# Window routing of a fused four-layer network: sums of the raw input, and the choice of key blocks moved into the qkv products

## The reference

```python
# xn = groupnorm of x with groups of 4 channels: xn = x * A + B, A and B per image and channel
proj = xw @ W_qkv + b_qkv                  # xw: xn in 7 x 7 windows of 8 x 8 pixels
q_win, k_win = mean of q, mean of k        # one vector of 128 per window: 49 x 128
lepe = depthwise_conv3x3(v_img) + lepe_b
logit = einsum('npc,nqc->npq', q_win * SCALE, k_win)      # 49 x 49
_, r_idx = top_k(logit, 4)                 # for each window the 4 windows whose keys it sees
attn = softmax(q * SCALE @ k[r_idx])       # 8 heads of 16 channels, 64 x 256 per window
out = (attn @ v[r_idx] + lepe) @ W_o + b_o
```

## Time and profile before

| | us |
|---|---|
| median of 3 runs | 3797.24 (3796.34 to 3798.78) |
| profiled execution | 3793.72 |
| its span (first to last instruction) | 3792.0 |
| PE busy | 3522.8 (93%) |
| DVE busy | 2374.0 (63%) |
| ACT busy | 2142.8 (57%) |
| POOL busy | 1655.4 (44%) |
| POOL L1508 idle before it, released by the DMA row<-ix | 303.6 |

### The profile page before, as it was taken

The page is one execution under the profiler, slowest core; times in us unless marked ns, Lnnn a source line. Parts: engine busy times, 40 slices in busy tenths (PEclk is TensorE's granted clock), DMA queues, the critical chain, the costliest instruction groups (busy, mean ns, idle before and its releaser), DMA issues. The chain is left out here.

```text
span 3792.0 us, 107529 instructions
## 1 busy us (share of the span) xinstructions
PE 3522.8 (93%) x31974; PEld 2993.2 (79%) x31974; DVE 2374.0 (63%) x6251; ACT 2142.8 (57%) x5921; POOL 1655.4 (44%) x2575
## 2 busy tenths in 40 slices
PE   6989898989989898969999999999999969979999
PEld 4656565656656565659999999999999969979998
DVE  4868687777868686853333333333333349988898
ACT  4969788787879797954443333333333324435554
POOL 2636364554636363730003333333334436646665
PEclk8999999999999999989999999999999989989999
DMA  6232222323132323211110000000002100000000
GB/s 213 71 96 74 90 80 75 87 61 110 49 113 58 108 63 98 73 66 50 50 55 1 0 0 0 0 0 0 0 6 61 61 26 1 1 14 35 35 35 34
DMA packets 202875, 194.44 MB, mean 51 GB/s; under 512 B 35744, under 2 KB 191136, under 8 KB 199456
## 3 DMA queue, kind: packets, MB, share of 16 engines
q1 hardware_dynamic: 171168, 177.15, 15.0%
q10 hardware_dynamic: 31360, 12.87, 1.2%
HBM read 123.30 MB, written 66.58 MB: 50 GB/s over the span
## 5 line engine op out<-in xcount | busy, mean ns | idle before, releaser
L196 PE MATMUL bank<-h,w_hh 128*128 128x128 f32 x8032 | 933.9, 275 | 0.0
L196 PEld LDWEIGHTS bank<-h,w_hh 128*128 128x128 f32 x8032 | 917.2, 192 | 0.0
L241 ACT ACTIVATE h<-bank,bg 128x128 f32<-128x128 f32 x1008 | 370.0, 367 | 818.7 <-PE bank L196 818.6
L1579 ACT ACTIVATE Pr<-bank,nmx 128x256 f32<-128x256 f32 x1568 | 722.6, 477 | 122.4 <-DVE nmx L1682 108.0
L1516 POOL TENSOR_TENSOR Pr<-Pr,rden 128x768 f32<-128x768 f32 x392 | 574.7, 1466 | 383.3 <-DVE rden L1749 383.3
L1682 DVE TENSOR_REDUCE nmx<-bank 128x1 f32<-128x256 f32 x1568 | 557.0, 416 | 210.1 <-PE bank L1854 206.4
L287 DVE SCALAR_TENSOR_TENSOR inp<-bank,b_in,tz 128x256 f32<-128x256 f32 x196 | 85.8, 479 | 698.2 <-ACT tz L224 698.2
L1508 POOL COPY kg<-kT 128x64 f32 x1568 | 312.6, 243 | 392.4 <-DMA row<-ix 303.6
L1865 PE MATMUL bank<-ident,Pr 128*128 128x128 f32 x3136 | 450.5, 285 | 3.7 <-POOL Pr L1516 2.1
L1588 ACT ACTIVATE PT<-bank 128x512 f32<-128x512 f32 x784 | 427.3, 604 | 39.7 <-PE bank L1865 36.6
L1854 PE MATMUL bank<-kg,qT 32*128 32x256 f32 x3136 | 399.8, 440 | 31.6 <-POOL kg L1508 22.9
(11 more groups left out here) (261 smaller groups left out, 6500.2 us busy)
## 6 DMA issues: line engine op xcount, KB each, us to landing
v_rows<-v_padded SPq DMA_DIRECT2D x168, 232.0 KB, 3.4
vg<-v_windows SPq DMA_DIRECT2D x1176, 32.0 KB, 2.1
first_gates<-gate_sums SPq DMA_DIRECT2D x28, 512.0 KB, 2.6
gate_sums<-first_gates SPq DMA_DIRECT2D x28, 512.0 KB, 3.5
v_padded<-vpad SPq DMA_DIRECT2D x56, 232.0 KB, 2.4
X<-in_x SPq DMA_DIRECT2D x8, 1568.0 KB, 15.1
vg<-v_windows ACTq DMA_DIRECT2D x392, 32.0 KB, 2.2
x_backup<-X SPq DMA_DIRECT2D x8, 1568.0 KB, 6.0
```

The source lines that it names most:

```text
L196: ins = pe.matmul(bank[m][:, tt * COLS:(tt + 1) * COLS], w_hh[:, k, m * 128:(m + 1) * 128], prev[:, k, :], start=False, stop=(k == NH - 1) ...
L241: act.activation(h[:, 2 * q + tt, m, :], bank[m][:, tt * COLS:(tt + 1) * COLS], ACT.Tanh, bias=bg[:, 0, m:m + 1]).then_inc(s_h, 1)
L1579: act.activation(Pr[:, par, j, :], bank[j][:, 0:KEYS], ACT.Exp, bias=nmx[:, par, j:j + 1], accum_out=den[:, par, j:j + 1])\
```

## The change

- The window sums are taken from the raw image X by DVE (into `xraw`), seven blocks in turns 0 to 3 (`SUMS_AT`), and made into sums of the normalised input by one operation with A and 64 B in turn 3. ACT no longer waits for the sum of a block before it overwrites `xb`.
- The two products of the sums stand in turn 4, in unused columns of the k and v banks, their bias additions on DVE in the same turn; the logits' product, scaling, top 8 and positions stand in turn 5.
- SP issues the DMA of the positions at the head of its turn 6.
- Behind the turns, lepe 0 waits only for block 5's evacuation; scores(0) stand ahead of lepe 1; on ACT the copy of lepe 1 stands behind the exps of window 0.
- `VAR_AT` is 41 instead of 40.

```diff
+            SUMS_AT = {0: (0, 1), 1: (2, 3), 2: (4, 5), 3: (6,)}
+            SUMS_BLOCK, LOGITS_BLOCK = 4, 5
-            MEAN_AT, VAR_AT = 39, 40
+            MEAN_AT, VAR_AT = 39, 41
...
 # SP, in the turns
+                            if b == LOGITS_BLOCK + 1:
+                                sp.wait_ge(s_tk, n * 3 + 4)
+                                sp.wait_ge(s_kg, (n * P2) + 1)
+                                sp.wait_ge(s_Tc, (n * P2) * 2 + 1)
+                                sp.dma_start(row[0:1, :], ix[:, 0:TOPK]).then_inc(s_row, 16)
...
 # ACT
-                            if b >= 2:
-                                act.wait_ge(s_qs, n * NBLK + b - 1)
...
+                        first_lepe(0)
...
                         exps(0, 0)
+                        first_lepe(1)
...
 # DVE, in the turns
-                            dve.wait_ge(s_xb, n * NBLK + b + 2)
-                            dve.tensor_reduce(xsum[:, b * NWIN:(b + 1) * NWIN], xb[:, par, :]
-                                              .rearrange("p (w k) -> p w k", k=W2), AXX, ALU.add).then_inc(s_qs, 1)
+                            for k in SUMS_AT.get(b, ()):
+                                dve.tensor_reduce(xraw[:, k * NWIN:(k + 1) * NWIN],
+                                                  xblk(n, k).rearrange("p (r w c) -> p w r c", r=ROWS, c=WIN),
+                                                  mybir.AxisListType.XY, ALU.add).then_inc(s_qs, 1)
+                            if b == SUMS_BLOCK - 1:
+                                dve.wait_ge(s_id, n * IN_DVE + IN_DVE)
+                                dve.tensor_scalar(B64[:], Bb[:, bass.ds(n, 1)], float(W2), None, ALU.mult).then_inc(s_xs, 1)
+                                dve.wait_ge(s_xs, n * 2 + 1)
+                                dve.wait_ge(s_qs, (n + 1) * NBLK)
+                                dve.tensor_scalar(xsum[:], xraw[:], A[:, bass.ds(n, 1)], B64[:, 0:1], ALU.mult, ALU.add)\
+                                    .then_inc(s_xs, 1)
...
+                            if b == SUMS_BLOCK:
+                                for i, sums in enumerate((qs, ks)):
+                                    dve.wait_ge(s_wp, n * 2 + 2)
+                                    dve.tensor_scalar(sums[:], bank[1 + i][:, BLK:BLK + P2], b64[:, i:i + 1], None, ALU.add)\
+                                        .then_inc(s_ws, 1)
+                            if b == LOGITS_BLOCK:
+                                dve.wait_ge(s_lg, n + 1)
+                                dve.tensor_scalar(lg[:], bank[6][0:P2, BLK:BLK + P2], QSCALE / (W2 * W2), None, ALU.mult)\
+                                    .then_inc(s_tk, 1)
+                                dve.wait_ge(s_tk, n * 3 + 2)
+                                dve.max(m8[:], lg[:]).then_inc(s_tk, 1)
                             dve.tensor_scalar(vpad[...], ...).then_inc(s_v, 1)
+                            if b == LOGITS_BLOCK:
+                                dve.wait_ge(s_tk, n * 3 + 3)
+                                dve.wait_ge(s_row, n * 16 + 16)
+                                dve.max_index(ix[:], m8[:], lg[:]).then_inc(s_tk, 1)
...
 # PE, in the turns: q product, then
+                            if b == SUMS_BLOCK:
+                                pe.wait_ge(s_xs, n * 2 + 2)
+                                pe.matmul(bk[:, BLK:BLK + P2], w_qkv[:, 0:C], xsum[:], start=True, stop=True).then_inc(s_wp, 1)
                             pe.matmul(bk[:, 0:BLK], w_qkv[:, C:2 * C], xs, start=True, stop=True).then_inc(s_pk, 1)
+                            if b == SUMS_BLOCK:
+                                pe.matmul(bv[:, BLK:BLK + P2], w_qkv[:, C:2 * C], xsum[:], start=True, stop=True)\
+                                    .then_inc(s_wp, 1)
+                            if b == LOGITS_BLOCK:
+                                pe.wait_ge(s_ws, n * 2 + 2)
+                                pe.matmul(bv[0:P2, BLK:BLK + P2], qs[:], ks[:], start=True, stop=True).then_inc(s_lg, 1)
...
 # PE, behind the turns
+                        pe.wait_ge(s_V, n * NBLK + NBLK)
                         for i in range(6):
                             lepe(0, i // 2, i % 2, bank[7])
...
+                        pe.wait_ge(s_v, n * NBLK + NBLK)
+                        pe.wait_ge(s_V, n * NBLK + NBLK + 1)
                         scores(0, 0)
+                        pe.wait_ge(s_tk, n * 3 + 2)
+                        for i in range(6):
+                            lepe(1, i // 2, i % 2, bank[6])
                         scores(1, 1)
```

More of the change, by code:

```diff
@@ L1251, in program @@
             s_vst = [sem("v_stored_even"), sem("v_stored_odd")]
-            s_qs, s_bq = sem("window_sums"), sem("query_bias_ready")
+            s_qs, s_bq = sem("raw_window_sums"), sem("query_bias_ready")
+            s_xs = sem("window_sums_scaled")
             s_wp, s_ws = sem("window_sums_product"), sem("window_sums_ready")
@@ L1278, in program @@
             b64 = sb("bias_sums", [C, 2])
+            xraw = sb("raw_sum", [C, P2])
             xsum = sb("window_sum", [C, P2])
+            B64 = sb("shift_sums", [C, 1])
             ident = sb("ident", [C, C])
@@ L1421, in _ @@
                                 passed(sp)
+                            if b == LOGITS_BLOCK + 1:
+                                sp.wait_ge(s_tk, n * 3 + 4)
+                                passed(sp)
+                                sp.wait_ge(s_kg, (n * P2) + 1)
+                                passed(sp)
+                                sp.wait_ge(s_Tc, (n * P2) * 2 + 1)
+                                passed(sp)
+                                sp.dma_start(row[0:1, :], ix[:, 0:TOPK]).then_inc(s_row, 16)
                             sp.wait_ge(s_v, n * NBLK + b + 1)
@@ L1436, in _ @@
                                     stack(n, b - 2, dy)
[L1438 to L1445, removed]
                         sp.wait_ge(s_vst[0], n * (STORED * 4) + STORED * 4 + 16)
@@ L1597, in _, with first_lepe @@
                         act.wait_ge(s_o, n * P2 + 1)
-                        for b in range(2):
+                        def first_lepe(b):
                             act.wait_ge(s_lp, n * NBLK + b + 2)
                             act.activation(by_row(lp[:, b, :]), bank[7 - b][:, 0:BLK], ACT.Copy).then_inc(s_le, 1)
+                        first_lepe(0)
                         act.wait_ge(s_vst[0], n * (STORED * 4) + STORED * 4 + 16)
@@ L1656, in image @@
                             dve.wait_ge(s_pv, n * NBLK + b + 1)
+                            if b == SUMS_BLOCK:
[8 more added lines that the diff above has]
+                                dve.wait_ge(s_tk, n * 3 + 2)
+                                passed(dve)
+                                dve.max(m8[:], lg[:]).then_inc(s_tk, 1)
                             dve.tensor_scalar(vpad[:, 1 + b * ROWS:1 + (b + 1) * ROWS, 1:1 + W],
@@ L1663, in image @@
                                 input_stats(dve, following(n), b)
[L1664 to L1676, removed]
                         def maxes(w, par):
@@ L1803, in image @@
                             ins.then_inc(s_pV, 1)
-                        pe.wait_ge(s_qs, (n + 1) * NBLK)
-                        pe.wait_ge(s_q, n * NBLK + NBLK)
-                        for i in range(2):
-                            pe.matmul(bank[0][:, i * P2:(i + 1) * P2], w_qkv[:, i * C:(i + 1) * C], xsum[:],
-                                      start=True, stop=True).then_inc(s_wp, 1)
-                        pe.wait_ge(s_V, n * NBLK + NBLK + 1)
-                        pe.wait_ge(s_v, n * NBLK + NBLK)
+                        pe.wait_ge(s_V, n * NBLK + NBLK)
                         def lepe(b, dx, h, to):
@@ L1840, in image @@
                             lepe(0, i // 2, i % 2, bank[7])
-                        pe.wait_ge(s_k, n * NBLK + NBLK)
-                        pe.wait_ge(s_ws, n * 2 + 2)
-                        pe.matmul(bank[1][0:P2, 0:P2], qs[:], ks[:], start=True, stop=True).then_inc(s_lg, 1)
-                        for i in range(6):
-                            lepe(1, i // 2, i % 2, bank[6])
-                        pe.wait_ge(s_tk, n * 3 + 2)
                         def scores(w, par):
```

1 line of the change is left out of this document (added).

## The result

| | before | after |
|---|---|---|
| median of the runs, us | 3796.79 (n 4) | 3752.85 (3752.41 to 3754.37, n 4) |
| ratio of the runs | | 0.9886, 95% interval [0.9869, 0.9904] |
| profiled execution, us | 3793.72 | 3752.41 |
| PE busy, us | 3522.8 (93%) | 3507.4 (94%) |
| POOL keys (L1508, after: L1513), idle before them, us | 392.4 | 341.3 |

44 us were gained where 50 had been forecast; 3752.9 lies in the range of 3734 to 3768. The spread of the runs of the kernel before over all comparisons was 3789 to 3805, that of the changed kernel 3749 to 3755.

A forecast was written before the change was run, and what follows sets the result against it. It took each first-stage image to be bound by a chain behind the qkv products (sums, logits, top-k, routes' DMA, keys, scores, exp). 43 (first exp) + 7 (clock) + 0 = 50 us, from 3797.2 to 3747, range 3734 to 3768.

The forecast's parts named there:

- Part 1: DVE, turns 0 to 3: seven strided sums of raw X at 0.62 us each, hidden under 1.3 us cover; costs nothing.
- Part 2: TensorE, turns 4 and 5: the moved sums' and logits' products are paid, turns end 1.0 us later, lepe 0 starts at once.
- Part 3: Routes' DMA moved on SP: leaves behind block 5's value stores; scores(0) 4.0 us after old sums' product start instead of 9.4.
- Part 4: First exp of each image: the last value store becomes last arrival; 5.65 us instead of 11.06, gaining 5.4 an image, 43.
- Part 5: Start of the windows: half clock behind the bubble goes; worth 1.4 us an image, holding in five images, 7 in all.
- Part 6: Turn 40: variance product a turn later ends TensorE's wait, which is parallel to DVE's; gain 0, moved product costs nothing.
- Rival A: Routes' DMA lands late behind a backlog of stores; only 3 us an image gained, 24 in all, 3773 us; chance 0.10.

The follow-up runs named there:

- e3: Changed kernel with the routes' DMA issued on SP behind the turns again, behind the last value stores: 3786.22 us.
- e6: Changed kernel with ACT's waits for the value stores and its first fetch behind the exps of window 0 instead of ahead: 3743.99 us.
- e4: Changed kernel with lepe 1 ahead of scores(0) on TensorE, as before the change: 3766.35 us.
- e7: As e6, plus scores(1) directly behind scores(0), ahead of lepe 1; ACT's first six windows written out, lepe 1's copy behind window 1's exps: 3767.28 us.
- e2: Kernel before the change with only the variance product moved to turn 41: 3795.85 us against 3796.02, ratio 0.9998.
- e5: Changed kernel with two operations of the mean's chain rewritten so neither has two SBUF tiles as inputs: 3743.77 us.
- e10: Changed kernel with the edits of e5 and e6 together: 3738.34 us, ratio to the kernel before 0.9841.
- e11: As e10 with e7's ACT order, and lepe 1 split, three pieces ahead of scores(1) and three behind: 3726.34 us, ratio to the kernel before 0.9811.
- e1: Changed kernel with the variance product back in turn 40: 3748.48 us.
- e12: Kernel before the change with only the two lines of e5 in the mean's chain: 3785.70 us against 3797.53, ratio 0.9965.
- e9: Changed kernel with every raw sum of X made twice on DVE, the first into a tile nobody reads: 3780.11 us.

## Why the prediction was right, and where it was off

- **Part 1** was right in its sum: a raw sum takes 0.607 us, and no TensorE wait appears in turn 4. The cover ahead of the sums' product is 1.57 us for 1.3; it had missed the narrower one of 0.93 in turn 0.
- **Part 2** was right where like stands beside like: image 4, with 3 us of half clock in its turns in both kernels, has them end 0.8 us later for a forecast 1.0. Lepe 0 follows without a gap.
- **Part 3**: routes at V-0.82, keys at V+2.04, scores(0) at V+2.85; foreseen E-0.2, E+3.2, E+4.0, that is V-1.2, V+2.2 and V+3.0 with V at E+1.0. Program order on SP decides, as said, and e3 shows the price, 33 us. The Trainium skill's rule of the ring order (DMA: Bandwidth & Descriptors, "Queues, rings and completion order") stayed without a cost in most images: 2.86 us from issue to keys in image 2, as with empty queues (2.84 in the earlier trace rows). In images 5 and 6 it was 3.4 and 3.8; over all profiles 10 of 80 images with the early issue have 3.4 to 3.9, and 2 of 32 with the late one 3.6 and 4.1, so that the stores in front are not shown to be the reason. The 0.6 that I added for the store in front was not there. Rival A did not happen.
- **Part 4**: first exp at V+4.97, foreseen V+4.65; the last arrival is the value store (e6). That 44.3 us were measured for 43 is luck in part: behind V the eight images gained 45.5, where 51 were foreseen (5.30 in the mean, 6.53 in image 0), and the turns grew by 1.2 in all instead of 8, since they ran 32 us at half clock instead of 44. No term had that. In the second profile of the changed kernel it is 41 us of half clock, and 43.1 gained.
- **Part 5**: 6.6 for 7 at the start of the windows; the clock held in six images, not five, and image 0 lost 2.6. Its mechanism carries more than I gave it: in e4 and e7 more is lost behind the first exp than ahead of it, and in e3 15 of 36 us. I had asked where the half clock would go, and not where it would come.
- **Part 6** is the step that failed. Its core was right: TensorE's wait is parallel to DVE's chain (e2, e5; 1.08 becomes 1.11), and the rule on the shared port in the Trainium skill (SBUF — State Buffer, "Who interferes with whom") fits the chain: with one input from PSUM the same operation takes 0.15 beside GpSimd. But "the moved product costs nothing" was argued from its own length alone, and no term asked what the clock does behind this turn. Turn 40 is the loosest turn of the loop, and the clock falls behind it in five to seven images of the changed kernel; windows 39 to 43 take 7.1 us more in the profile (9.5 in the second) where 0 was foreseen. The stretches are there with the product in either turn. With it in turn 40 the kernel is 2.5 to 4.4 us faster, of which these windows show 1.9; in the kernel before, the same move costs nothing that could be measured (e2).
- The middle of the windows, 2.8 us slower, had no term in the sum. The loss sits at one place of ACT's loop; why the queue pauses there stays open.

## What to carry to other kernels

When a late chain is moved forward, look for the one instruction whose place in an in-order queue holds it: here one DMA on SP was worth 33 of 44 us, once its data were ready early. Price every hole in TensorE's work twice, once as a wait and once as a fall of the clock on the work behind it, and put work that has to be done anyway into the holes: lepe 1 inside the hole kept the clock, as a block (e10) and in halves (e11), and ran at half speed behind it (e7). And where an engine's wait goes away, look for what it waits for next in the same turn before counting anything.

## What the runs showed of the hardware

- The clock can fall with no hole as long as the 2.73 us of the earlier trace rows: behind turn 40 TensorE had been busy 3.59 of 4.9 us, with one hole of 1.11 (changed kernel), and 3.89 of 5.1 with one of 1.08 (e1). With e5's two lines (e5, e10, e11, e12) none of the 28 images with a mean has a stretch there. Whether it falls depends on more than the hole: with it, the two profiles of the changed kernel have 5 and 7 images with a stretch, e1 6, e4 5, e6 3, e2 2, e3, e7 and e9 one each, and the kernel before none with the same 1.08.
- A DVE difference of one column takes 1.06 us beside a GpSimd product with both inputs in SBUF and 0.15 with one in PSUM; the term with two column scalars takes 0.27 in the same place (e5).
- DVE idles 5.7 us at the back edge of its loop in every profile but e9's, and 7.0 to 7.1 there, with seven instructions more in the body. The Trainium skill (Runtime: NRT & Kernel Launch, "Instruction fetch mechanics") says that a taken branch to code outside the fetched pages stalls for the fetch; the row names no releaser, and nothing here shows more than the idle.
